# First layer of tiles 4 to 7 moved in between the feed-forward steps of tiles 0 to 3, with the gate in three groups

## What is computed

```python
# layer 0: u = v = fside of the batch (128 x 16), b = cond of the batch
z = ((x @ v) / 128) @ u.T / 16
x = x + gelu(x @ W.T + fc_bias + z + b, approximate=False)
# layer 1: the gate
gate_in = concat(mean over all tokens, mean over head+proprio, mean over wrist+proprio)
logits = (gate_in @ gate_w + gate_b) * (1 + scale(cond)) + shift(cond)
w_be = the two largest softmax scores of each batch, renormed, 0 elsewhere
# layer 1: experts; expert 1 leaves out the wrist tokens, expert 2 the head tokens
out = sum over e of w_be[:, e] * mask[e] * (gelu(x @ ew1[e] + eb1[e], approximate=True) @ ew2[e] + eb2[e])
shared = gelu(x @ sw1 + sb1, approximate=True) @ sw2 + sb2
x = x + out + shared
```

## Time and profile before

| | |
|---|---|
| median of three runs | 278.51 us (277.38 to 280.41) |
| the profiled execution | 276.86 us, of which the trace spans 275.1 us |
| TensorE busy | 246.1 us (89%), 1207 products |
| VectorE busy | 193.1 us (70%) |
| ScalarE busy | 146.3 us (53%) |
| GpSimd busy | 22.1 us (8%) |
| mean granted TensorE clock | 0.972 |
| chain that ended last | TensorE 71%, ScalarE 13%, VectorE 12%, issue 3% |
| ScalarE, approximated GELU into h | 160 of 653 ns mean, 94.9 us |
| VectorE, low halves of the gated steps | 128 of 658 ns mean, 76.3 us |

### The profile page before, as it was taken

The page is one execution under the profiler, slowest core; times in us unless marked ns, Lnnn a source line. Parts: engine busy times, 40 slices in busy tenths (PEclk is TensorE's granted clock), DMA queues, the critical chain, the costliest instruction groups (busy, mean ns, idle before and its releaser), DMA issues.

```text
span 275.1 us, 3381 instructions
## 1 busy us (share of the span) xinstructions
PE 246.1 (89%) x1207; PEld 205.0 (75%) x1207; DVE 193.1 (70%) x414; ACT 146.3 (53%) x273; POOL 22.1 (8%) x39
## 2 busy tenths in 40 slices
PE   7999947589589999899989998999899989999963
PEld 6788845258377798778867886888688858899852
DVE  0128997999999495659556873877297729779861
ACT  4159947995061863384348335733664375563600
POOL 5000000095000900000000000000000000000000
PEclk9999977999959999999999999999999999999998
DMA  6998000000000010001000100010001000100101
GB/s 124 155 184 280 1 1 2 0 0 0 0 2 0 0 39 3 0 0 38 2 1 0 38 2 0 0 39 2 0 0 38 2 0 0 38 2 2 38 0 38
DMA packets 15756, 7.40 MB, mean 27 GB/s; under 512 B 6120, under 2 KB 14460, under 8 KB 15740
## 3 DMA queue, kind: packets, MB, share of 16 engines
q1 hardware_dynamic: 14726, 6.98, 10.8%
q10 hardware_dynamic: 854, 0.18, 0.3%
q0 software_dynamic: 160, 0.02, 0.1%
HBM read 5.09 MB, written 2.10 MB: 26 GB/s over the span
## 4 chain that ended last, share of the span: by engine, by line
PE 71%; ACT 13%; DVE 12%; issue 3%; DVEq 0%; POOL 0%; ACTq 0%; POOLq 0%
PE ps L391 20%; PE ps L393 19%; PE ps L392 19%; ACT h L329 6%; DVE hs_lo L601 4%; ACT hs_hi L332 4%; PE ps L420 3%; DVE hs_hi L596 3%; PE ps L430 3%; PE ps L404 2%; PE ps L412 2%; DVE W_lo L580 1%; PE ps L479 1%; PE ps L397 1%; ACT h L315 1%
## 5 line engine op out<-in xcount | busy, mean ns | idle before, releaser
L329 ACT ACTIVATE h<-ps,b_col 128x512 f32<-128x512 f32 (+1 forms) x160 | 94.9, 653 | 68.0 <-PE ps L393 61.1
L391 PE MATMUL ps<-x_hi,W_hi 128*128 128x512 f32 (+1 forms) x160 | 63.6, 398 | 16.3 <-ACT hs_hi L332 12.5
L601 DVE SCALAR_TENSOR_TENSOR hs_lo<-h,w_be,hs_hi 128x512 fp32r<-128x512 f32 (+1 forms) x128 | 76.3, 658 | 0.0
L596 DVE TENSOR_SCALAR hs_hi<-h,w_be 128x512 fp32r<-128x512 f32 (+1 forms) x128 | 48.7, 444 | 22.0 <-PE ps L393 21.5
L391 PE MATMUL ps<-hs_hi,W_hi 128*128 128x512 f32 (+1 forms) x160 | 59.0, 369 | 2.7 <-DVE hs_lo L601 2.5
L393 PE MATMUL ps<-x_lo,W_hi 128*128 128x512 f32 (+1 forms) x160 | 59.8, 374 | 0.0
L392 PE MATMUL ps<-x_hi,W_lo 128*128 128x512 f32 (+1 forms) x160 | 59.7, 373 | 0.0
L393 PE MATMUL ps<-hs_lo,W_hi 128*128 128x512 f32 (+1 forms) x160 | 58.6, 366 | 0.0
L392 PE MATMUL ps<-hs_hi,W_lo 128*128 128x512 f32 (+1 forms) x160 | 58.4, 365 | 0.0
L391 PEld LDWEIGHTS ps<-x_hi,W_hi 128*128 128x128 f32 x160 | 30.9, 193 | 30.5 <-ACT hs_hi L332 22.6
L590 DVE TENSOR_TENSOR hs_lo<-h,hs_hi 128x1024 fp32r<-128x1024 f32 x16 | 20.0, 1294 | 29.4 <-ACT hs_hi L332 29.4
(11 more groups left out here) (92 smaller groups left out, 151.2 us busy)
## 6 DMA issues: line engine op xcount, KB each, us to landing
W_raw<-in_L_cond_ew SPq DMA_DIRECT2D x8, 256.0 KB, 7.4
out<-x_tok SPq DMA_DIRECT2D x8, 256.0 KB, 2.3
x_tok<-in_x SPq DMA_DIRECT2D x2, 336.0 KB
W_raw<-in_L_cond_sw SPq DMA_DIRECT2D x2, 256.0 KB, 7.0
x_tok<-in_x SPq DMA_DIRECT2D x1, 352.0 KB
x_tok<-in_x SPq DMA_DIRECT2D x2, 168.0 KB
x_tok<-in_x SPq DMA_DIRECT2D x3, 84.0 KB
x_tok<-in_x SPq DMA_DIRECT2D x2, 88.0 KB
```

Source lines behind the costliest of these rows:

```text
L329: ins = nc.scalar.activation(span(h[:, k % 3, c, :], s), up_bank(k, c), ACT.Gelu_apprx_tanh, bias=b1_col[:, s, c:c + 1])
L391: nc.tensor.matmul(dst, w_hi, m_hi, start=start, stop=False)
L596: nc.vector.tensor_scalar(hs_hi[:, k % 2, :, c], h[:, k % 3, :, c], w_be[:, t * NB + b, s - 1:s], None, ALU.mult).then_inc(hi_ok, 1)
L601: nc.vector.scalar_tensor_tensor(hs_lo[:, k % 2, :, c], h[:, k % 3, :, c], w_be[:, t * NB + b, s - 1:s], f32(hs_hi[:, k % 2, :, c]), ALU.m ...
```

## The change

The prologue goes over tiles 0 to 3 only (`NA = 4`). The loads of x and fside for tiles 4 to 7 are two chunks at the end of SP's queue, behind all weights. Layer 0 of tile t = 4 to 7 is placed by the helper `late_tile(k, place)`: it counts from the first expert step f of tile t-4 (f = 2, 7, 12, 17). In TensorE's loop `transpose_F(t)` stands between up(f+2) and down(f), `xT(t)` behind down(f), `matrices(t)` behind down(f+1), `layer0(t)` behind down(f+2). In ScalarE's loop both copies stand behind gelu(f+2), `gelu0_late(t)` behind gelu(f+4), which is step (t-2, 0), and `x1_high(t)` behind gelu(f+6). In VectorE's loop `matrix(t)` stands behind split(f+2), `residual(t)` behind split(f+4), the sums of two tiles behind split(f+5) of the odd one, `x1_low(t)` behind split(f+6). All four PSUM uses of a late tile go one after the other through bank 7, which the output transposes and the logits use too; the waits say who has it. The SBUF scratch is in the raw weights that have been split by then.

The gate has three groups, tiles 0 to 3, 4 and 5, 6 and 7 (`GATES`); the two late ones are placed by `late_gate` in the same manner, from f = 12 and f = 22. gate_in at f+1, logits behind down(f+3), gate_logits behind split(f+4), gate_weights behind split(f+6), output_biases behind split(f+7), gate_tanh behind gelu(f+7).

```diff
-    CHUNKS = [(0, 1), (1, 2), (2, 4), (4, 8)]
+    CHUNKS = [(0, 1), (1, 2), (2, 4), (4, 6), (6, 8)]
-    HB = B // 2
+    NA = 4
+    GATES = [(0, 4), (4, 6), (6, 8)]
...
+        def late_tile(k, place):
+            for t in range(NA, NT):
+                if first_step(t - NA) + place == k:
+                    return t
+            return None
...
+            def fT_late_copy(t):
+                act.wait_ge(fT_ps, t + 1)
+                act.wait_ge(w_lo_ok, made(2))
+                act.wait_ge(M_ps, t)
+                nc.scalar.activation(fT_late, psLate[0:R, :].rearrange("p (b d) -> p b d", d=D), ACT.Copy
                                      ).then_inc(fT_ok, 1)
+            def gelu0_late(t):
+                nc.scalar.activation(table_probe[:, 1:2], table_probe[:, 0:1], ACT.Gelu)
+                act.wait_ge(y_ps, t + 1)
+                act.wait_ge(w_lo_ok, made(1))
+                act.wait_ge(x1_ok, t)
+                for b in range(NB):
+                    ins = nc.scalar.activation(g0_late[:, b * L:(b + 1) * L], psLate[:, b * L:(b + 1) * L],
+                                               ACT.Gelu, bias=bias0[:, t * NB + b:t * NB + b + 1])
+                ins.then_inc(g0_ok, 1)
...
 # ScalarE
-            for t in range(NT):
-                if t + 2 < NT:
+            for t in range(NA):
+                if t + 2 < NA:
                     xT_copy(t + 2)
                     fT_copy(t + 2)
                 gelu0(t)
                 if t >= 1:
                     x1_high(t - 1)
-                if t >= 4:
-                    weight_high(WEIGHTS[t - 4])
-            x1_high(NT - 1)
-            gate_tanh(0)
+                if t >= 2:
+                    weight_high(WEIGHTS[t - 2])
+            x1_high(NA - 1)
+            weight_high(WEIGHTS[2])
             act.wait_ge(b1_in, 32)
             gelu(0)
-            for n in WEIGHTS[4:7]:
-                weight_high(n)
+            gate_tanh(0)
+            weight_high(WEIGHTS[3])
             gelu(1)
-            for n in WEIGHTS[7:]:
+            for n in WEIGHTS[4:6]:
                 weight_high(n)
             for k in range(2, K):
                 gelu(k)
-                if k == 3:
-                    gate_tanh(1)
+                if k in (2, 3):
+                    for n in WEIGHTS[2 * k + 2:2 * k + 4]:
+                        weight_high(n)
...
+                t = late_tile(k, 2)
+                if t is not None:
+                    fT_late_copy(t)
+                    xT_copy(t)
+                t = late_tile(k, 4)
+                if t is not None:
+                    gelu0_late(t)
+                t = late_tile(k, 6)
+                if t is not None:
+                    x1_high(t)
+                g = late_gate(k, 7)
+                if g is not None:
+                    gate_tanh(g)
...
 # TensorE
             def out_transpose(t):
                 pe.wait_ge(outT_ok, NSEG * (t + 1))
-                if t >= 1:
+                if first_step(t) in gate_blocks:
+                    pe.wait_ge(logit_read, gate_blocks[first_step(t)] + 1)
+                elif t + NA < NT:
+                    pe.wait_ge(g0_ok, t + NA + 1)
+                else:
                     pe.wait_ge(out_tok_ok, t)
...
+            pe.wait_ge(eb2T_read, NSEG)
+            pe.wait_ge(mod_terms_ok, 1)
+            nc.tensor.matmul(psMod, ones[:, :], mod_terms[:, :, :], start=True, stop=True).then_inc(mod_ps, 1)
             up(0)
+            logits(0)
             up(1)
             for k in range(K):
                 if k + 2 < K:
                     up(k + 2)
+                t = late_tile(k, 0)
+                if t is not None:
+                    transpose_F(t)
                 down(k)
-                if k == 1:
-                    logits(1)
+                if t is not None:
+                    xT(t)
+                t = late_tile(k, 1)
+                if t is not None:
+                    matrices(t)
+                t = late_tile(k, 2)
+                if t is not None:
+                    layer0(t)
+                g = late_gate(k, 3)
+                if g is not None:
+                    logits(g)
...
 # VectorE, from tile 1 of the prologue on
+                if t == 1:
+                    segment_sums(0, 2)
                     time_gate()
-                if t == 3:
                     output_rows()
...
+            weight_low(WEIGHTS[0])
+            segment_sums(2, 4)
+            gate_in(0)
+            dve.wait_ge(bias_in, 16 * 3)
+            modulation()
+            x1_low(NA - 1)
             gate_logits(0)
-            x1_low(NT - 1)
+            weight_low(WEIGHTS[1])
             weight_low(WEIGHTS[2])
+            split(0)
+            gate_weights(0)
             weight_low(WEIGHTS[3])
-            gate_weights(0)
+            split(1)
+            weight_low(WEIGHTS[4])
             output_biases(0)
-            split(0)
-            weight_low(WEIGHTS[4])
-            gate_in(1)
             weight_low(WEIGHTS[5])
-            split(1)
-            split(2)
-            weight_low(WEIGHTS[6])
-            weight_low(WEIGHTS[7])
-            for k in range(3, K):
+            for k in range(2, K):
                 t, s = STEPS[k - 2]
                 if s == NS - 1:
                     out_sum(t)
...
                 split(k)
...
+                if k in (2, 3):
+                    weight_low(WEIGHTS[2 * k + 2])
+                    weight_low(WEIGHTS[2 * k + 3])
+                t = late_tile(k, 2)
+                if t is not None:
+                    matrix(t)
+                t = late_tile(k, 4)
+                if t is not None:
+                    residual(t)
...
```

160 lines of the change are left out of this document (94 added, 66 removed).

## The result

The changed kernel took **280.6 us** (median of 20 executions, 277.59 to 282.27), the kernel before 277.85 us on the same chip (20 executions, 274.48 to 280.63). The ratio is **1.0112, 95% interval 1.0077 to 1.0147**: about 1.1% slower. Ratios leave slow executions out, which leaves one to three in experiments 2, 6 and 8 and five of twelve in experiment 4, so there the median of all is read beside the ratio, or instead of it. The profiled execution of after took 280.86 us, span 279.1, mean clock 0.941 (before: 276.86, 275.1, 0.972). It is 4.0 us longer.

The account below looks back on a forecast made before the run. VectorE's queue bounds the ramp, TensorE the steady blocks. Ramp -15.3, inserted products +6.3, table switches +8.0 and gates +1.9 give +0.9 on 276.86: 277.8, or 279.4 us on the median's scale; range 274.5 to 285.5.

Parts of the forecast that it names:

- no change: Whole kernel: measured time between 275.7 and 281.3 us, within about 1% (2.8 us); chance 0.41.
- slower: Whole kernel: measured time above 281.3 us; chance 0.4.
- Release of the chain: Prologue: with tiles 4 to 7 out, up(0) starts at 32.1 instead of 41.3, gate_logits(0) at 36.7 (35.2 to 38.2).
- Vector chain: Ramp, VectorE: gate_logits(0) to end of split(2) takes 22.1 us instead of 23.4; bounds 1 less, 1.5 more.
- TensorE from down(2) to down(4): Ramp behind split(2): TensorE needs 13.8 us, so down(4) ends at 72.6 instead of 87.88, 15.3 us gained.
- Rival B: Ramp: clock falls at down(2) after 2.6 us of idle, costing 2.6, gate_logits(0) 1.5 later; 283.5 us; chance 0.22.
- Table switch: Blocks, ScalarE: each late tile's two table loads delay gelu(7) and up(8), 2.0 us a tile, 8.0 in all.
- Rival D: Late tiles' eight table switches: a wait of 1.38 us beside each load; 290.4 us; chance 0.06.
- layer0 at nothing: Blocks: layer0(t), 0.89 us, hides in TensorE's hole before up(7)'s second chunk; uncovered it is 3.6.
- Inserted products: Blocks, TensorE: late tiles' transposes and matrices cost 2.11 us a tile, 6.3 for tiles 5 to 7.
- Rival E: Four blocks: split(7)'s cover fails, a second idle after gelu(7), layer0 not hidden; 285.4 us; chance 0.07.
- Gates: Later blocks: gate 4-5 holds 0.3 us, gate 6-7 holds 1.6 via out_sum(4) before down(26); together 1.9.

Follow-up runs that it names:

- experiment 2: Kernel after with the probe repeated (Gelu, tanh form, Gelu), two more table switches per late tile; median 300.23 us of four beside 276.45, 1.086.
- experiment 6: Kernel after with gate_logits(1) and gate_logits(2) moved from in front of out_sum to behind it; ratio 0.990, median of all six 279.64 us.
- experiment 8: Kernel after with 14 and 11 unread fp32 products in TensorE's idle before layer0(3) and up(0); ratio 0.992 from three of ten, median of all 278.0 us.
- experiment 4: Same as experiment 3 plus a one-element tanh-form gelu behind the pieces of gelu0_late; ratio 0.997 from five of twelve, median of all 278.93 us.
- experiment 5: Kernel after with output_biases(0) moved from behind split(1) to behind split(4), GpSimd's first twelve bias adds moving with it; ratio 0.994.
- experiment 3: Kernel after with late tiles' matrices ahead of down(f+1), layer 0 behind it, gelu0_late ahead of gelu(f+4); ratio 1.019.
- experiment 1: Kernel after with the tanh form of GELU in the late tiles' layer 0 and no probe, so no table switch; ratio 0.989.
- experiment 7: Kernel after with 34 and 26 unread fp32 products in TensorE's idle stretches before layer0(3) and up(0); ratio 1.027.
- experiment 9: Kernel before with gate_tanh(1) moved from behind gelu(3) to behind gelu(5); ratio 0.990.
- experiment 10: Kernel before with gate 4-7's work and output_biases(0) moved out of the first block, layer 0 left in the prologue; ratio 0.991.
- experiment 11: Kernel after with experiment 4, experiment 5 and experiment 6 together, late gates' weights and biases two places later; ratio 0.984, median 272.92 us.
- experiment 12: Experiment 11 plus the 14 and 11 unread products of experiment 8, against the kernel before; ratio 0.967, median 269.43 us.

## Why the prediction was right or wrong

Predicted 279.4 with a range of 274.5 to 285.5; measured 280.6. The forecast was 0.9 us more than before's 278.51; measured against before's median of twenty, 277.85, it is 2.7 more. So 0.7 of the closeness is the luck of the scale. The ratio's interval of 0.8% to 1.5% slower straddles the 1% that I had called the limit between "no change" (0.41) and "slower" (0.40). The mechanism was right. By its steps, on the profiled execution:

- **Release of the chain.** up(0) predicted 32.1, measured 32.50. gate_logits(0) predicted 36.7 between 35.2 and 38.2, measured 38.13. It is the upper end, and for the reason that was given for it: a low clock, and up(0) ahead of the logits. That cost 1.4 us here. The middle was still the right choice, as the eight profiles with this code have 35.05 to 38.56, 36.8 in the mean.
- **Vector chain.** Predicted 22.1, measured 21.7 (38.13 to 59.8). This was right by two errors that cancel: split(2) is 0.9 slower under GpSimd's adds, which I had carried over unchanged, and split(0), split(1) are 0.8 faster without them (2.35 each instead of 2.62 and 2.85). The upper bound of 1.5 for this was the better warning: experiment 5 got 2.8 us out of it.
- **TensorE from down(2) to down(4).** Predicted 13.8, measured 13.97. Rival B's fall of the clock at down(2) did not come in this execution: 0.47 and 0.40 for its products after 2.38 us of idle. It did come in three others with the same code at this place. In the profiles of experiments 2 and 6 the first product of down(2) takes 0.76 and 0.77 us after 3.23 us of idle, the clock stays at 0.50 for some 5 us, and the first mark comes 17.4 and 17.5 us behind down(2)'s start instead of 14.8. That is the 2.6 that rival B was priced at. In experiment 8 it came after 2.38 us of idle (0.50 from 54 to 56 us) and cost 1.6. Experiment 3 idled 3.25 us there and kept the high clock. So rival B was right in mechanism, place and price, for some executions; that the profiled one escaped it is luck. The ramp gained 13.9, not 15.3.
- **Table switch.** up(8) was to end 11.35 after down(4); down(6) starts right behind it at 85.27, which is 11.33. Price 2.0, which experiment 1 confirmed. Rival D's drain is refuted: the Trainium skill's page "ScalarE: Activation LUTs", section "What ACT_TABLE_LOAD costs", would have 1.38 us of drain beside each load. Here 1.28 us of load stand with at most 0.03 of pause, in after and in the doubled switches of experiment 2. The measurement decides.
- **layer0 at nothing.** Right: hidden in the hole. Moved out of it, it cost 0.9 (experiment 4).
- **Inserted products.** 2.11 a tile for tiles 5 to 7; blocks 1 and 2 grew by 4.1 with the switch, as the sum has it. Rival E's second idle is not there: the 1.53 us is the only wait over 0.2 in these two blocks.
- **Gates.** 0.3 and 1.6 predicted, 0.3 and 1.9 measured. Right, but the 0.3 depends on the table's stall (experiment 1).
- **What the sum did not hold.** 1.5 us of low clock in block 4, behind a 1.53 us stall. The same stall in blocks 1 and 2 was not followed by it, nor was the one of block 4 in the profiles of experiments 5, 6, 7 and 8 (28.6 us each, as summed). It is rival B's mechanism at a place that it did not name.

So the 3.1 us that the execution is over the predicted 277.8 are 1.4 of the ramp, 1.5 of clock in block 4 and 0.3 in block 5. The twenty executions of after differ largely by the clock: their spans run from 275.8 to 280.5, about 1.5 us shorter for each 0.01 of mean clock, with a correlation of -0.76.

What stays open: what makes the clock fall in one execution and not in the next at the same stall, and the low clock near the very end in the profiles of experiments 1, 4 and 6 to 12, where the rest after the last mark is 1.3 to 2.5 us longer than in before, after and experiments 2, 3 and 5.

## What to carry to other kernels

Work laid between steady steps is paid in full, except for what fits an existing hole. Price each inserted item by the row of the engine that it lands on, and look which wait is late next before you count on the gain. A table load is made by the instruction that needs it, behind that instruction's wait, so give a cheap early instruction of the same function the load. A start of the chain that varies by 3 us between executions hides a gain of 2, so compare the stretches behind it and not the totals. Look at what another engine runs beside the queue that bounds you: moving work that nobody waits for can be worth more than the restructuring.

## What the runs showed of the hardware

- VectorE is slower while GpSimd adds on tiles in SBUF: four 128x512 operations with one tensor input take 1.66 us alone and 2.3 to 2.5 beside the adds, four with two tensor inputs 2.73 and 3.59. When experiment 5 moved the adds, the longer times moved with them.
- A table load takes 1.28 us with no pause around it at each of the late tiles' eight switches; with a one-element probe 1.50.
- A load is not made ahead of time: ScalarE stood 3.6 us free before it in experiment 3.
- An fp32 product of 128x128x128 costs 0.23 us at the high clock, in two passes of 0.115 (5.97 us for 52 at a granted clock of 1.00, experiment 7). The 68 passes that took 8.64 us there began at 0.50.
- TensorE's clock can fall for 3 us behind a 1.5 us stall in a stretch that is otherwise full, in one execution and block and not in others. At down(2) it fell in three of eight profiles with the same code there: after idles of 3.23, 3.23 and 2.38 us, and not after 3.25, 2.38, 2.37, 2.36 and 1.66. Mean clocks of one kernel's executions lay between 0.931 and 0.959.
